# Feeding the first pair through the quantising path tile by tile, with other release points, fillers and a reordered tail, in an attention and FP4 feed-forward kernel

## The reference

```python
q, k, v = (LN(x) @ Wq + bq), (ctx @ Wq + bq), (ctx @ Wq + bq)       # 16 columns each
corr = mean over batch and head of real(ifft(fft(q) * conj(fft(k))))  # 128 lags
w, shift = softmax(top_k(corr, 12))
R = sum_i w_i * roll(v, -shift_i)                                     # one set of lags for all tiles
x = x + broadcast(R) @ Wout + bout
xn = LN(x)
g, u = fp4(xn) @ fp4(w_gate).T, fp4(xn) @ fp4(w_up).T                 # 704 columns each
x = x + fp4(silu(g) * u) @ fp4(w_down).T
# fp4(): blocks of 16 columns, scale = max|.|/6, values snapped to {0,.5,1,1.5,2,3,4,6}
```

## Time and profile before

| | before |
|---|---|
| three timed runs, median | 476.21 us (474.34 to 478.40) |
| the profiled execution | 476.25 us, span 474.4 us |
| mean granted TensorE clock | 0.985 |
| the same from 11.9 to 23.7 us (second of the page's 40 slices) | 0.7 |
| busy: PE, DVE, ACT, POOL | 94%, 92%, 86%, 53% |

### The profile page before, as it was taken

One profiled execution on the slowest core, in us unless ns is written; L12 is line 12 of the kernel. 1 busy time (PEld: TensorE's weight loads), 2 busy tenths in 40 slices (PEclk: granted clock), 3 DMA queues, 4 the chain that ended last, 5 costly groups with the idle time before them and its releaser, 6 DMA issues.

```text
span 474.4 us, 9954 instructions
## 1 busy us (share of the span) xinstructions
PE 445.0 (94%) x3383; PEld 296.4 (62%) x3383; DVE 435.9 (92%) x758; ACT 405.8 (86%) x699; POOL 251.6 (53%) x340
## 2 busy tenths in 40 slices
PE   4599997978699999999999999999999999999997
PEld 4587886834366566666566666666666665666686
DVE  3699988569999999999999999999999999999893
ACT  3379979679989999999999999999999999987674
POOL 4157763354466665566655555666666666433300
PEclk9799999989999999999999999999999999999999
DMA  7999901442256667666566666656657665555562
GB/s 242 337 347 347 352 19 33 92 105 51 49 116 138 138 128 150 139 132 132 129 128 129 128 139 138 141 130 139 139 118 140 139 138 116 121 121 118 118 140 72
DMA packets 161971, 67.95 MB, mean 143 GB/s; under 512 B 126336, under 2 KB 161664, under 8 KB 161920
## 3 DMA queue, kind: packets, MB, share of 16 engines
q1 hardware_dynamic: 161920, 67.31, 60.6%
HBM read 27.38 MB, written 9.18 MB: 77 GB/s over the span
## 4 chain that ended last, share of the span: by engine, by line
DVE 48%; PE 26%; issue 17%; DMA 5%; SPq 1%; ACT 1%; POOL 1%; DVEq 1%; ACTq 0%; POOLq 0%
DVE hb L1266 9%; DVE y_h L1379 8%; DVE bm L1385 6%; DVE ctx_sb L1271 6%; PE ps L990 4%; DVE bm L1409 4%; PE ps L960 3%; PE ps L961 3%; PE ps L962 3%; DVE bm L1404 3%; DVE x_c L1058 2%; DVE x_t L1054 2%; PE ps L993 2%; PE ps L814 2%; PE ps L791 2%
## 5 line engine op out<-in xcount | busy, mean ns | idle before, releaser
L960 PE MATMUL ps<-guT_hi,a_xT 128*128 128x512 f16 (+1 forms) x384 | 140.1, 365 | 8.4 <-DVE hb L1266 5.3
L961 PE MATMUL ps<-guT_lo,a_xT 128*128 128x512 f16 (+1 forms) x384 | 140.2, 365 | 0.0
L962 PE MATMUL ps<-guT_hi,a_xT 128*128 128x512 f16 (+1 forms) x384 | 140.1, 365 | 0.0
L990 PE MATMUL ps<-dT_hi,hqT 128*128 128x256 f16 x704 | 124.7, 273 | 0.5 <-ACT hqT L676 0.5
L993 PE MATMUL ps<-dT_lo,hqT 128*128 128x256 f16 x384 | 87.4, 273 | 0.0
L520 POOL TENSOR_TENSOR ctx_sb<-w_q_lo,sl 128x704 f16<-128x704 f16 x58 | 87.2, 1525 | 0.0
L990 PEld LDWEIGHTS ps<-dT_hi,hqT 128*128 128x128 f16 x704 | 68.9, 98 | 10.6 <-ACT hqT L676 0.6
L651 ACT ACTIVATE w_raw<-ps,inv_gu 128x704 f32<-128x704 f32 x64 | 53.8, 840 | 21.1 <-PE ps L962 20.9
L536 POOL TENSOR_TENSOR sl<-bm,sh 128x240 f16<-128x240 f32 (+2 forms) x34 | 20.6, 606 | 95.4 <-DVE y_h L1379 72.7
L960 PEld LDWEIGHTS ps<-guT_hi,a_xT 128*128 128x128 f16 x384 | 37.9, 99 | 44.3 <-DMA a_xT<-ctx_sb 9.6
L962 PEld LDWEIGHTS ps<-guT_hi,a_xT 128*128 128x128 f16 x384 | 37.8, 99 | 39.3 <-issue 1.4
(11 more groups left out here) (176 smaller groups left out, 816.6 us busy)
## 6 DMA issues: line engine op xcount, KB each, us to landing
xs<-in_x_dram SPq DMA_DIRECT2D x16, 512.0 KB, 8.7
ctx_sb<-in_ctx_dram SPq DMA_DIRECT2D x16, 512.0 KB, 8.2
out_dram<-a_xT SPq DMA_DIRECT2D x64, 128.0 KB, 2.3
w_raw<-a_scratch SPq DMA_DIRECT2D x60, 128.5 KB, 2.7
hqT<-ctx_sb SPq DMA_TRANSPOSE x62, 3.7
w_raw<-in_L_ffn_w_down_dram SPq DMA_DIRECT2D x1, 704.0 KB, 8.2
w_raw<-in_L_ffn_w_gate_dram SPq DMA_DIRECT2D x1, 640.0 KB, 5.1
w_raw<-in_L_ffn_w_up_dram SPq DMA_DIRECT2D x1, 640.0 KB, 6.4
```

Source lines behind the costliest of these rows:

```text
L960: pe.matmul(dst, xt[:, c, :], guT[0][:, c, n0:n1], start=(c == 0), stop=False)
L961: pe.matmul(dst, xt[:, c, :], guT[1][:, c, n0:n1], start=False, stop=False)
L962: last = pe.matmul(dst, xt[:, KC + c, :], guT[0][:, c, n0:n1], start=False, stop=(c == KC - 1))
L990: last = pe.matmul(dst, hqT[:, j % 4, c, :], dT_hi[:, c, :], start=(c == 0 and not late and not preset(j)), stop=(c == DCH - 1 and j > 0))
```

## The change

Five parts, in the order of the program.

1. PE runs 18 filler products (results unused) ahead of the transposes of the third load step. Ahead of the first gate product it runs 8 fillers in place of 20, and waits for the end of `keep_attn` behind them in place of ahead of them.
2. The first pair goes through the x path one tile at a time, with semaphores of its own (`f_...`) for tile 0, and is turned by two DMAs of four blocks (`turn_first`) in place of one of eight. SP loads the rows of pairs 2 and 3 ahead of these; three of the four stores of the attention blocks stand between them. The last evacuation of gate and up weights on ACT moves behind the squares. The addition for pair 2 waits until both tiles' products are done.
3. POOL's low scale no longer waits for `yx_done`. The addition of the stages from 2 on waits for DVE's high product of h in place of L1058.
4. Tiles 0 and 56 to 61 get opened and preset as the others; tiles 58 and 59 in banks 0 and 1. `ident_out` and its products go.
5. In the tail, of the low products of h that DVE made for pairs 29 and 30, the second tile's goes to POOL. SP stores tile 57 between the two turns of pair 30 in place of ahead of them. ACT takes tiles 60 and 61 out before it copies the last turned pieces.

```diff
@@ SP
-            store_attn(1)
             load_attn(2)
-            store_attn(2)
-            store_attn(3)
             load_attn(3)
+            turn_first(0)
+            for g in range(1, 4):
+                store_attn(g)
+            turn_first(1)
...
+            def turn_first(t):
+                sp.wait_ge(of_tile(t, "f_grid", "x4_steps"), K_XQ)
+                sp.dma_start_transpose(xqT[:, 0, 4 * t:4 * t + 4, :], xq[:, 0, t].rearrange("p w n -> p (w n)")
+                                       ).then_inc(xT[0] if t else s["f_turned"], 16)
@@ POOL
+            stats_first(0)
+            stats_first(1)
+            low_scales_first(0)
...
                 if 2 <= st < NP:
                     pool.wait_ge(s["yh_done"], st - 1)
-                    pool.wait_ge(s["yx_done"], min(st + 2, NP))
                     low_scales(st - 1)
...
+                if st == -3:
+                    low_scales_first(1)
+                    pool.wait_ge(s["x4_steps"], K_XQ)
...
-                    if st >= 1:
+                    if st >= 2:
+                        pool.wait_ge(s["h4_steps"], K_HQ * (st - 1))
+                    elif st == 1:
                         pool.wait_ge(s["x4_steps"], K_XQ * (st + 1) + 2)
...
                     for t in range(2):
+                        pool.wait_ge(s["z_lo"], 1 + 2 * t)
+                        low_h(NP - 3 + t, (1,))
                         last_low_scales(t)
@@ ACT
+            square_first(0)
+            square_first(1)
+            evacuate_weights(act, range(GU_FILLS - 1, GU_FILLS))
+            normalise_first(0)
+            normalise_first(1)
+            scale_high_first(0)
+            split_first(0)
+            square_x(1)
+            scale_high_first(1)
+            split_first(1)
...
                     residual(2 * NP - 8)
+                    preset_x(2 * NP - 6)
+                    preset_x(2 * NP - 5)
                     last_split(0)
                     residual(2 * NP - 7)
+                    preset_x(2 * NP - 4)
+                    preset_x(2 * NP - 3)
                     residual(2 * NP - 6)
                     residual(2 * NP - 5)
                     last_split(1)
+                    residual(2 * NP - 4)
+                    residual(2 * NP - 3)
                     keep_turned(0)
                     keep_turned(1)
-                    residual(2 * NP - 4)
                     keep_turned(2)
                     keep_turned(4)
-                    residual(2 * NP - 3)
@@ PE
+                if i == W_FIRST:
+                    filler(18)
...
-            pe.wait_ge(s["t_steps"], 14)
+            pe.wait_ge(s["t_steps"], 11)
...
-            for _ in range(20):
+            for _ in range(8):
...
+            pe.wait_ge(s["t_steps"], 14)
...
-                if late:
-                    pe.matmul(dst, ident_out[:, :], xs[:, j, :], start=True, stop=False)
@@ DVE
-            add_head(0)
-            keep_attn(0)
-            add_head(1)
...
                     if st == NP - 1:
                         high_h(p)
-                        low_h(p)
+                        turned_product(p, 0, 1).then_inc(s["z_lo"], 1)
...
-                    for t in range(2):
-                        turned_products(p, t)
+                    turned_product(p, 0, 0)
+                    turned_product(p, 0, 1).then_inc(s["z_lo"], 1)
+                    turned_product(p, 1, 0).then_inc(s["z_lo"], 1)
```

More of the change, by code:

```diff
@@ L259, in tile_of, with x_cols, x_runs, of_tile @@
             return w.rearrange("p (ih t r) -> p t ih r", ih=IH, t=2)[:, t]
+        def x_cols(t):
+            return slice(RUN_H + t * NBX, RUN_H + (t + 1) * NBX)
+        def x_runs(t):
+            return slice(2 * RUN_H + t * RUN_X, 2 * RUN_H + (t + 1) * RUN_X)
+        def of_tile(t, first, regular):
+            return (s[first], s[regular])[t]
         def pair_ok(n):
@@ L270, in preset @@
         def preset(i):
-            return i >= 2 and i % 4 != 1 and i // 2 < NP - 4
+            return not added(i) and 0 <= i < 2 * NP - 2
         def n_added(i):
@@ L428, in _ @@
                     turn_h(2 * st - 6)
+                    if st == NP + 1:
+                        store(2 * st - 9)
                     turn_h(2 * st - 5)
@@ L433, in _ @@
                     store(2 * st - 7)
-                if pair_ok(st + 1):
+                if st >= 0 and pair_ok(st + 1):
                     turn_x(st + 1)
-                if tile_ok(2 * st - 7) and st != NP + 1:
+                if tile_ok(2 * st - 7) and st not in (NP, NP + 1):
                     store(2 * st - 7)
@@ L844, in turn_v, with filler @@
                 last.then_inc(s["v_tr"], 1)
+            def filler(n):
+                for _ in range(n):
+                    pe.matmul(bank(5)[:, 0:P], ones[:, :], ident[:, :], start=True, stop=True)
             for i in range(NQ):
+                if i == W_FIRST:
+                    filler(18)
                 for u in range(2):
@@ L872, in _ @@
             pe.wait_ge(s["evc"], 2 * NQ)
-            def filler(n):
-                pe.wait_ge(s["v_ev"], 2)
-                for _ in range(n):
-                    pe.matmul(bank(5)[:, 0:P], ones[:, :], ident[:, :], start=True, stop=True)
             def transpose_weights(f):
@@ L966, in down @@
                 final = j // 2 == NP - 1
-                late = j >= 2 * (NP - 4) and not final
-                dst = bank(2 * (1 - j % 2) if final else 6 + j % 2)[:, 0:D]
+                dst = bank(down_bank(j))[:, 0:D]
                 if final:
                     if j % 2 == 0:
+                        out_ready(pe, 2 * NP - 5)
                         turn_last(0)
@@ L989, in down @@
                             pe.wait_ge(s["z_ev"], 4 if c else 3)
-                    last = pe.matmul(dst, hqT[:, j % 4, c, :], dT_hi[:, c, :], start=(c == 0 and not late and not preset(j)),
-                                     stop=(c == DCH - 1 and j > 0))
+                    last = pe.matmul(dst, hqT[:, j % 4, c, :], dT_hi[:, c, :], start=(c == 0 and not preset(j)),
+                                     stop=(c == DCH - 1))
                     if c < LOCH:
                         pe.matmul(dst, hqT[:, j % 4, c, :], dT_lo[:, c, :], start=False, stop=False)
-                if j == 0:
-                    last = pe.matmul(dst, ident_out[:, :], xs[:, j, :], start=False, stop=True)
                 last.then_inc(s["d_done"], 1)
@@ new lines, in grid_first @@
+            def grid_first(t):
+                done = of_tile(t, "f_grid", "x4_steps")
+                c, tt = tile_of(x_c[:, :], t), tile_of(x_t[:, :], t)
+                dve.wait_ge(of_tile(t, "f_split", "x_split"), 3)
+                offset(c, tt).then_inc(done, 1)
+                dve.wait_ge(done, 1)
+                grid(c, tt).then_inc(done, 1)
+                dve.wait_ge(done, 2)
+                for part, scale in ((0, sh), (1, sl)):
+                    if part:
+                        dve.wait_ge(of_tile(t, "f_sl", "sl"), 1)
+                    dve.tensor_tensor(xq[:, 0, t, part, :].rearrange("p (ih r) -> p ih r", ih=IH), c.bitcast(F16),
+                                      scale[:, 0, x_runs(t)].unsqueeze(1).broadcast_to([P, IH, RUN_X]), ALU.mult).then_inc(done, 1)
@@ new lines, in _ @@
+            add_first(0)
+            add_first(1)
+            keep_attn(0)
+            largest_first(0)
+            scales_first(0)
+            inverses_first(0)
+            scaling_first(0)
+            add_head(1)
+            largest_first(1)
+            scales_first(1)
+            grid_first(0)
+            inverses_first(1)
+            scaling_first(1)
+            for g in range(1, 4):
+                keep_attn(g)
+            grid_first(1)
+            largest_x(1)
+            for st in range(-1, END):
```

168 lines of the change are left out of this document (122 added, 46 removed).

## The result

The changed kernel takes 469.16 us (median of 4, 468.10 to 470.62) against 476.28 us (4 runs) for the kernel before: ratio 0.985, 95% interval 0.980 to 0.990. The prediction was 468.7 us. The profiled execution took 469.22 us with a span of 467.4 us, 7.0 us less than before.

What follows compares the result with a forecast made beforehand. DVE was taken as the bound, PE about 0.3 us a stage behind. Middle 4.6 + turn 1.9 + tail 1.2 = 7.7 us, 7.5 kept: 468.7 us from 476.25, range 465.8 to 473.5.

Steps and rivals of the forecast that it cites:

- What bounds the kernel: Middle stages: DVE never waits and its work sets each stage, 11.30 us; PE stands about 0.3 us a stage behind.
- Middle stages, 4.6 us: Stages 2 to 26: earlier release of POOL's addition saves 0.24 us without residual, 0.12 with; 4.6 us in all.
- The low scale, 0: Middle stages: without `yx_done` POOL's low scale gains some 0.2 us, but nothing waits for POOL; 0.
- The power operation: Slower rival, middle stages: POOL's power operation precedes DVE's L1054, each stage grows by up to 0.6 us; 484; chance 0.07.
- Phase 1, 0: Start: 18 fillers finish transposes about 2 us sooner, but DVE waits for a load of x; 0, at most 0.5.
- The turn, 1.9 us: First pair: without PE's waits DVE's second `gate_up` comes at 105.7 in place of 107.66; 1.9 us, bounds 0 and 3.0.
- the turn does not gain: Rival, first pair: second pair's addition now waits for tile 1; 470.5 us; counted within the forecast's 0.73, no own chance.
- The tail, 1.2 us: End: fewer `ident_out` products and earlier turns; last pair turned at 464.8, not 466.0; 1.2 us, bounds 0.3 and 1.9.

Runs made afterwards that it cites:

- yx_back: The changed kernel with POOL's wait on `yx_done` ahead of the low scale put back; one execution, 468.49 us.
- pair_old: The changed kernel with the first pair taken the old way: both tiles together, one turn, 20 fillers; 469.19 us, ratio 0.984.
- rel_back: The changed kernel with POOL's addition of stages 2 to 26 again released by DVE's second x difference; 474.17 us, ratio to before 0.994.
- pool_free: The changed kernel without POOL's wait for tile 1's products ahead of pair 2's addition, plus 12 fillers ahead of tile 6; 468.01 us, ratio 0.983.
- before_warm: The kernel before with 32 fillers in place of 20 ahead of the first gate product; 475.30 us, ratio 0.9982.
- rel_early: The changed kernel with POOL's addition released one DVE operation earlier, by the h difference; one execution, 490.09 us.
- add_mid: The changed kernel with POOL's addition moved between the two tiles' low products, without a wait on DVE; 484.04 us, ratio 1.014.
- both_turn: The changed kernel with tile 0's turn issued only when tile 1's products are there too; one execution, 473.71 us.

## Why the prediction was right, and where it was not

- **What bounds the kernel**: right. DVE's own work sets each middle stage in every variant, from 10.79 to 12.17 us, except in the long stage, where DVE waited 0.50 us for ACT; PE followed down to 21.97 us for two stages.
- **Middle stages, 4.6 us**: right in mechanism and nearly in size. The stages were forecast at 11.06 and 11.18 and are 11.03 and 11.18; alone, the release gave 4.82 us. In the profile of after 0.6 of it went into the one long stage, behind gate products at half clock that the prediction did not have, and 0.2 into a stage of 11.26 us whose cause was not traced. A detail was off: I took a loss of 0.28 us for DVE's product, with POOL's hold counted from the moment at which DVE lets go; counted from POOL's recorded start it would be 0.18. It is 0.24, between the two.
- **The rule of the Trainium skill** (GPSIMD Engine Reference, Key points: contention with DVE instructions of two SBUF inputs) agrees with the traces for POOL's large operations: DVE's operations with two SBUF operands were held, those with one operand or with one in PSUM were not. The runs also show who waits beside these: the one that comes second, so the new start on top of L1163 cost DVE nothing (0.42 us as before) and lengthened POOL's addition from 1.18 to 1.24 us.
- **The low scale, 0**: right, by yx_back. **The power operation**, the slower rival: refuted. It starts ahead of DVE's L1159 in after (262.12 against 262.19), as the rival had it, and L1159 keeps its 0.88 us. So this small operation (128x2), although it came first, held nothing.
- **Phase 1, 0**: right. In after itself the fillers ran past the landing of the load and saved PE 0.1 us, not the 2 us that I had. Where they did save about 2 us (pair_old, rel_back), 0.2 to 0.3 was left at the reduction, inside the "at most 0.5".
- **The turn, 1.9 us**: the table's 2.24 agrees with it and proves little. The steps were forecast well: tile 0 scaled at 87.82 (87.9), POOL's second-pair addition at 93.20 (93.3), pair 3 normalised at 102.14 (102.4), `gate_up` at 105.43 (105.7). But they were set against a profile of before whose first gate products ran at half clock, and that the table agrees is the luck of having compared with the same execution. The step that failed is that I took ACT's waits for PE at the two silus (2.00 and 0.61 us) for a property of the kernel: in the same code at full clock they are 0.33 and nothing. Against before at full clock the tile-wise way gives 0.71 us. I had the row with products of 0.61 us where 0.38 is usual and did not look at the granted clock of that stretch. The 0.71 is nearer to the 0 of the rival "the turn does not gain" than to 1.9, though the rival's reason, the addition that waits for tile 1, was worth only the half microsecond of pool_free.
- **The tail, 1.2 us**: right in its steps, too large. DVE's two `gate_up` rows behind stage 31's follow after 9.97 and 6.74 us, 10.24 and 7.05 before: 0.58 us, where 0.4 was forecast. But the last turning begins only 0.87 us sooner, not 1.2. These rows of after show why (PE, then SP and POOL):

```profile
457.05 0.27 PE L1084 MATMUL ps<-dT_hi,hqT 128*128 128x256 f16 x1 [0.32 <-DMA hqT<-ctx_sb]
...
458.90 0.78 PE L1097 MATMUL ps<-ident,ctx_sb 128*128 128x128 f16 x11
```

```profile
453.36 1.40 SPq L418 DMA_TRANSPOSE hqT<-ctx_sb  x1
```

```profile
451.54 1.53 POOL L545 TENSOR_TENSOR ctx_sb<-w_q_lo,sl 128x704 f16<-128x704 f16 x1 [0.90 <-DVE ctx_sb L1430]
```

Tile 61's turn is now the late one. It is issued at 453.36, in the old time (6.22 us more) 459.6 and not 459.2, because POOL's low product had to wait for DVE's (it begins at 451.54, in the old time 457.8 and not 457.5), and PE starts on it 3.7 us later. Behind the last turning another 0.1 us is lost.

Seen by medians, the change gains 7.1 us. The release alone gave 4.6 by medians and 4.8 by the profiles; the tail is 0.8 in the profiles. For the rest, about 1.5 us, the profiles offer 0.7 for the tile-wise turn, and 0.8 by difference for first gate products that are no longer at half clock in part of the executions (before_warm gained 0.85 us by its median). This split is not shown: pair_old has neither of the two, should by it be 1.5 us slower than the changed kernel, and its median is 469.19 us against 469.16, with intervals of 1.6 and 2.3 us either way.

## What to carry to other kernels

Where GpSimd and VectorE share a stage, place each large GpSimd operation by what VectorE does behind its start, give it a stretch of one-operand or PSUM work, and ask what it pushes back; here the right release brought 4.8 us, and one instruction further cost 20.9. Before an edit is priced against a wait for TensorE, read the granted clock of that stretch: behind a wait of 3 us one execution here had the full clock and another had not. Agreement of a total with its forecast is no proof of its terms; a run with one part alone is.

## What the runs showed of the hardware

- GpSimd's addition of 128x512 in f32 (1.18 to 1.25 us long) keeps a two-operand VectorE operation out until 1.11 us after its start in before and rel_early (512 and 1408 columns), 1.17 to 1.19 in after and 1.04 in pool_free (256 columns); its f16 product of 128x704 (1.53 us) until 1.40 us after its start (add_mid). A reduction (1.62 us) and `gate_up` with one PSUM operand (1.80 for two) beside them keep their durations to 0.01 us.
- GpSimd's power operation on 128x2 took 1.24 us when it started 0.21 us behind a two-operand VectorE operation (before), and its usual 0.70 when it started 0.07 us ahead of the same one (after); VectorE's took 0.88 us both times.
- TensorE's granted clock differs between executions behind the same wait in the same code: DVE's first sum came 0.8 to 1.0 us later behind the first product of L935 in 4 of 14 profiles (pair_old, rel_back, pool_free, both_turn), though PE's wait for the load of cT just ahead was the same 0.6 to 0.7 us in all of them. The 17 executions of before that were timed beside before_warm, on one chip, fall into groups too: 474.1 to 475.0 us at a mean clock of 0.992 or 0.993, 475.8 to 476.9 at 0.985 or 0.986, 476.6 to 478.2 below.
